# A twelve-layer decoder kernel: in the first cross attention, the output product and the second half's query projection as three one-pass products each, with the weights and the latents split by GpSimd

## What is computed

```python
x = _layernorm(x + _L0_attn_ref(...), axis=-1)
x = _layernorm(x + _L0_xattn_ref(ctx_1024, x, gamma_media, beta_media, gamma_lat, beta_lat, Wq, bq, Wkv, bkv, Wo, bo), axis=-1)
x = _layernorm(x + _L0_ffn_ref(x, router_w, w13, w2), axis=-1)      # mixture of 8 experts
```

## Time and profile before

| | before |
|---|---|
| three runs, median | 920.63 us (918.99 to 921.9) |
| profiled execution | 912.8 us, span 910.9 us |
| TensorE busy | 856.6 us, 94% |
| VectorE busy | 662.2 us, 73% |
| ScalarE busy | 572.5 us, 63% |
| GpSimd busy | 307.3 us, 34% |
| granted TensorE clock, mean | 0.989 |

### The profile page before, as it was taken

How to read it: one execution, slowest core, us unless ns; L and a number is a source line. 1 busy time by engine, 2 the same in 40 slices (tenths; PEclk the granted TensorE clock), 3 DMA queues, 4 the chain that set the end, 5 groups by cost and what they waited for, 6 DMA issues and landing times.

```text
span 910.9 us, 14508 instructions
## 1 busy us (share of the span) xinstructions
PE 856.6 (94%) x4558; PEld 561.4 (62%) x4578; DVE 662.2 (73%) x1175; ACT 572.5 (63%) x1080; POOL 307.3 (34%) x296
## 2 busy tenths in 40 slices
PE   8999999999899888989899879999999999999997
PEld 4576644776535543445545546776357888888884
DVE  3576626777779769659768766563368999999996
ACT  5356624665557556468677732334667888888886
POOL 0111004674038400019438526434001344444330
PEclk9999999999999998999999999999999999999999
DMA  9000000113000000000000061403009999999981
GB/s 358 25 1 0 0 1 18 38 50 118 0 1 2 1 1 0 1 0 2 2 0 2 2 259 52 139 24 99 1 29 217 239 245 240 244 241 244 239 222 60
DMA packets 28721, 77.82 MB, mean 85 GB/s; under 512 B 4432, under 2 KB 11856, under 8 KB 28208
## 3 DMA queue, kind: packets, MB, share of 16 engines
q1 hardware_dynamic: 27520, 74.74, 29.3%
q0 software_dynamic: 1152, 2.44, 0.8%
HBM read 72.50 MB, written 6.28 MB: 86 GB/s over the span
## 4 chain that ended last, share of the span: by engine, by line
PE 71%; DVE 16%; ACT 10%; issue 2%; DMA 1%; SPq 0%; POOL 0%; another core or an unknown queue 0%; DVEq 0%; ACTq 0%; POOLq 0%
PE ps L839 10%; PE ps L841 9%; PE ps L840 9%; PE ps L611 4%; PE ps L1228 4%; PE ps L601 3%; PE ps L624 3%; PE ps L291 2%; PE ps L1246 2%; ACT arena L1948 2%; PE ps L1550 2%; PE ps L228 2%; PE ps L1632 2%; PE ps L1603 1%; DVE arena L771 1%
## 5 line engine op out<-in xcount | busy, mean ns | idle before, releaser
L839 PE MATMUL ps<-parts 128*128 128x512 f32 x416 | 166.6, 401 | 4.0 <-DVE ps L2563 1.5
L841 PE MATMUL ps<-parts 128*128 128x512 f32 x416 | 162.1, 390 | 0.0
L840 PE MATMUL ps<-parts 128*128 128x512 f32 x416 | 161.9, 389 | 0.0
L869 ACT ACTIVATE parts<-ps 128x512 fp32r<-128x512 f32 x192 | 115.2, 600 | 54.1 <-PE ps L841 24.6
L873 DVE TENSOR_TENSOR parts<-ps,parts 128x512 fp32r<-128x512 f32 x192 | 132.5, 690 | 7.2 <-ACT parts L869 1.2
L857 POOL TENSOR_TENSOR parts<-ring,zeros 128x1024 fp32r<-128x1024 f32 (+2 forms) x36 | 51.1, 1419 | 183.1 <-PE ps L841 142.2
L2563 DVE TENSOR_TENSOR ps<-ps,arena 128x512 f32<-128x512 f32 x156 | 108.2, 694 | 3.0 <-DMA arena<-m_comb 2.1
L839 PEld LDWEIGHTS ps<-parts 128*128 128x128 f32 x416 | 78.2, 188 | 24.9 <-DVE parts L873 3.4
L2097 ACT ACTIVATE ps<-ps 128x512 f32<-128x512 f32 x156 | 90.8, 582 | 2.8 <-PE ps L841 0.4
L841 PEld LDWEIGHTS ps<-parts 128*128 128x128 f32 x416 | 78.1, 188 | 16.7
L840 PEld LDWEIGHTS ps<-parts 128*128 128x128 f32 x416 | 78.1, 188 | 16.0 <-issue 0.5
(11 more groups left out here) (479 smaller groups left out, 1535.7 us busy)
## 6 DMA issues: line engine op xcount, KB each, us to landing
arena<-m_comb SPq DMA_DIRECT2D x156, 256.0 KB, 4.7
ring<-m_in SPq DMA_DIRECT2D x20, 512.0 KB, 5.5
arena<-m_in SPq DMA_DIRECT2D x4, 1408.0 KB
pack<-pack_in SPq DMA_DIRECT2D x1, 2058.5 KB, 10.3
ring<-m_up_in SPq DMA_DIRECT2D x8, 256.0 KB, 2.7
slots_x<-empty_in SPq DMA_DIRECT2D x1, 1584.1 KB, 7.8
pack<-pack_in SPq DMA_DIRECT2D x1, 1187.0 KB, 14.8
pack<-pack_in SPq DMA_DIRECT2D x1, 1149.5 KB, 12.5
```

The costliest lines, as they stand in the source:

```text
L839: nc.tensor.matmul(dst, w_high, x_high, start=start, stop=False, skip_group_check=True)
L840: nc.tensor.matmul(dst, w_high, x_low, start=False, stop=False, skip_group_check=True)
L841: return nc.tensor.matmul(dst, w_low, x_high, start=False, stop=stop, skip_group_check=True)
L869: nc.scalar.activation(m_hh[0:rows, p], ps[0:rows, src, :], ACT.Copy).then_inc(R(t, "_hh"), 1)
```

## The change

Both products go through `mm3`. New float32r tiles are laid over the arena: `x_wo` for the split of `x_m` and later of `x_u` (8 high blocks, 8 low blocks), and sixteen `x_outs`, each with the high and low part of one head and one half of the attention output; the first of them holds the split latents of half 1 before that.

- GpSimd, before its other work: high and low part of `x_m` (two instructions of 128 x 1024), then of the latents of half 1 (two of 128 x 512). After its last copy in the wave loop: high and low part of `x_u` (two of 128 x 1024).
- TensorE: `x_project(1, ...)` and the output product issue three one-pass matmuls in place of each float32 one. The projection waits for the fourth GpSimd split, the output product for the sixth, and each of its 16 units for its own low part.
- ScalarE: 16 copies to high parts, three of them inside the last loop body, the others after it. VectorE: 16 subtractions to low parts after the loop, the bias copy after the sixth, and `center_outputs` after them all.
- The semaphore `a_zeros` of a later layer becomes the seventh count of `mid_pool`.

The diff, cut to its core: the tiles, TensorE's two products, ScalarE's high parts, VectorE's low parts, and GpSimd's splits before its first copies and after its loop.

```diff
+        x_outs = [rounded(f"x_out_{u}", (21600, 8192)[u >= 4] + T * (u % 4 if u < 4 else u - 4), T) for u in range(2 * XH)]
+        x_wo = rounded("x_wo", 25696, 2 * XH * P)
...
             def x_project(p, heads):
                 pe.wait_ge(S("norm_out"), 3 + p)
+                if p == 1:
+                    pe.wait_ge(S("mid_pool"), 4)
...
-                    mm(bank(4 + n % 4), x_m[:, h, :], x_kv[:, HB * p:HB * (p + 1), 1, :], start=True, stop=True).then_inc(S("x0_qmm"), 1)
+                    if p == 0:
+                        ins = mm(bank(4 + n % 4), x_m[:, h, :], x_kv[:, 0:HB, 1, :], start=True, stop=True)
+                    else:
+                        ins = mm3(bank(4 + n % 4), x_wo[:, h * P:(h + 1) * P], x_wo[:, (XH + h) * P:(XH + h + 1) * P],
+                                  half(x_outs[0], 0), half(x_outs[0], 1), True, True)
...
-            pe.wait_ge(S("x0_o"), 2 * B + 2)
+            pe.wait_ge(S("mid_pool"), 6)
             for p in range(2):
                 for h in range(XH):
-                    ins = mm(bank(p), x_u[:, h, :], half(x_q[:, h, :], p), start=False, stop=(h == XH - 1), skip_group_check=True)
+                    u = XH * p + h
+                    pe.wait_ge(S("x0_u"), 3 + u)
+                    ins = mm3(bank(p), x_wo[:, h * P:(h + 1) * P], x_wo[:, (XH + h) * P:(XH + h + 1) * P], half(x_outs[u], 0), half(x_outs[u], 1),
+                              False, h == XH - 1)
...
+                    elif k == 2:
+                        x_out_high(0)
+                        x_out_high(1)
+                    else:
+                        x_out_high(2)
...
+            def x_out_high(u):
+                act.wait_ge(S("x0_o"), 2 * B + 5 if u >= XH else B + 2)
+                A_(half(x_outs[u], 0), x_out(u), ACT.Copy).then_inc(S("x0_o"), 1)
...
+            for u in range(3, 2 * XH):
+                if u == 4:
+                    act.wait_ge(S("mid_pool"), 6)
+                x_out_high(u)
...
+            for u in range(2 * XH):
+                dve.wait_ge(S("x0_o"), x_out_copies(u))
+                V.tensor_tensor(half(x_outs[u], 1), x_out(u), half(x_outs[u], 0), ALU.subtract).then_inc(S("x0_u"), 1)
...
+            pool.wait_ge(S("x0_m"), 1)
+            G.tensor_tensor(x_wo[:, 0:XH * P], x_mflat, zeros[:, 0:1].to_broadcast([P, XH * P]), ALU.add).then_inc(S("mid_pool"), 1)
+            pool.wait_ge(S("mid_pool"), 1)
+            G.tensor_tensor(x_wo[:, XH * P:2 * XH * P], x_mflat, x_wo[:, 0:XH * P], ALU.subtract).then_inc(S("mid_pool"), 1)
+            pool.wait_ge(S("norm_out"), 4)
+            G.tensor_tensor(x_parts[0], x_last, zeros[:, 0:1].unsqueeze(2).to_broadcast([P, HB, P]), ALU.add).then_inc(S("mid_pool"), 1)
+            pool.wait_ge(S("mid_pool"), 3)
+            G.tensor_tensor(x_parts[1], x_last, x_parts[0], ALU.subtract).then_inc(S("mid_pool"), 1)
...
+            pool.wait_ge(S("x0_u"), 1)
+            G.tensor_tensor(x_wo[:, 0:XH * P], x_flat, zeros[:, 0:1].to_broadcast([P, XH * P]), ALU.add).then_inc(S("mid_pool"), 1)
+            pool.wait_ge(S("mid_pool"), 5)
+            G.tensor_tensor(x_wo[:, XH * P:2 * XH * P], x_flat, x_wo[:, 0:XH * P], ALU.subtract).then_inc(S("mid_pool"), 1)
```

More of the change, by code:

```diff
@@ L694, in narrow_values_scalar @@
             waits(act, t)("_vproj", 1)
-            act.wait_ge(S("a_zeros"), 1)
+            act.wait_ge(S("mid_pool"), 7)
             for p in range(2):
@@ L836, in hidden_bank, with x_out_copies, x_out @@
             return 6 + p if j < lead else 4 + 2 * (j % 2) + p
+        def x_out_copies(u):
+            return 2 * B + 1 + u + int(u >= 2) + int(u >= 3)
+        def x_out(u):
+            return half(x_q[:, u % XH, :], u // XH)
         def mm3(dst, w_high, w_low, x_high, x_low, start, stop):
@@ L1549, in x_project @@
                         pe.wait_ge(S(f"x0_q{n % 2}"), n // 2 - 1)
-                    mm(bank(4 + n % 4), x_m[:, h, :], x_kv[:, HB * p:HB * (p + 1), 1, :], start=True, stop=True).then_inc(S("x0_qmm"), 1)
+                    if p == 0:
[3 more added lines that the diff above has]
+                                  half(x_outs[0], 0), half(x_outs[0], 1), True, True)
+                    ins.then_inc(S("x0_qmm"), 1)
             def x_turn_inputs(p):
@@ L2241, in _ @@
             x_body(B // 2 - 1, True)
-            dve.wait_ge(S("x0_mw"), 5)
-            V.tensor_copy(bo, ps[:, 4, 0:4]).then_inc(S("bo"), 1)
+            for u in range(2 * XH):
+                dve.wait_ge(S("x0_o"), x_out_copies(u))
+                V.tensor_tensor(half(x_outs[u], 1), x_out(u), half(x_outs[u], 0), ALU.subtract).then_inc(S("x0_u"), 1)
+                if u == 5:
+                    dve.wait_ge(S("x0_mw"), 5)
+                    V.tensor_copy(bo, ps[:, 4, 0:4]).then_inc(S("bo"), 1)
             def center_outputs():
@@ L2605, in x_keys_values @@
                 G.tensor_copy(x_kvts[:, slot], x_kvt[:, bass.ds(b, 1), :, :].rearrange("p o s d -> p (o s) d")).then_inc(S("x0_kvts"), 1)
+            x_mflat = x_m.rearrange("p h d -> p (h d)")
+            pool.wait_ge(S("x0_m"), 1)
+            G.tensor_tensor(x_wo[:, 0:XH * P], x_mflat, zeros[:, 0:1].to_broadcast([P, XH * P]), ALU.add).then_inc(S("mid_pool"), 1)
+            pool.wait_ge(S("mid_pool"), 1)
+            G.tensor_tensor(x_wo[:, XH * P:2 * XH * P], x_mflat, x_wo[:, 0:XH * P], ALU.subtract).then_inc(S("mid_pool"), 1)
+            x_last = x_kv[:, HB:B, 1, :]
+            x_parts = [half(x_outs[0], k).rearrange("p (b t) -> p b t", b=HB) for k in range(2)]
+            pool.wait_ge(S("norm_out"), 4)
+            G.tensor_tensor(x_parts[0], x_last, zeros[:, 0:1].unsqueeze(2).to_broadcast([P, HB, P]), ALU.add).then_inc(S("mid_pool"), 1)
+            pool.wait_ge(S("mid_pool"), 3)
+            G.tensor_tensor(x_parts[1], x_last, x_parts[0], ALU.subtract).then_inc(S("mid_pool"), 1)
             for k in range(2):
@@ L2622, in _ @@
                     x_keys_values(2 * i + slot, slot)
+            pool.wait_ge(S("x0_u"), 1)
+            x_flat = x_u.rearrange("p h d -> p (h d)")
+            G.tensor_tensor(x_wo[:, 0:XH * P], x_flat, zeros[:, 0:1].to_broadcast([P, XH * P]), ALU.add).then_inc(S("mid_pool"), 1)
+            pool.wait_ge(S("mid_pool"), 5)
+            G.tensor_tensor(x_wo[:, XH * P:2 * XH * P], x_flat, x_wo[:, 0:XH * P], ALU.subtract).then_inc(S("mid_pool"), 1)
             mix_gpsimd(pool, "m0", xT, M0_CH, M0_ROWS, lambda: pool.wait_ge(S("y_ready"), 4))
             pool.wait_ge(S("y_ready"), 6)
-            G.memset(a_vflat, 0.0).then_inc(S("a_zeros"), 1)
+            G.memset(a_vflat, 0.0).then_inc(S("mid_pool"), 1)
             narrow_sums_gpsimd(pool, "x1")
```

## The result

The changed kernel took 924.3 us (median of 7 runs, 918.61 to 925.41), the kernel before, on the same chip, 920.53 us (7 runs, 918.99 to 921.9). The ratio is 1.0040 (95% interval 1.0024 to 1.0056): the change costs 2 to 5 us. Its profiled execution took 925.41 us, with a span of 923.6 us and a mean granted clock of 0.984. In a later set of runs the same kernel came to 1.0021 (1.0001 to 1.0042). Of the predicted gain of 4.3 us, 4.1 came; the loss was 6.5 us in the changed layer where 3.8 were predicted.

What follows compares the result with a forecast made beforehand. TensorE, with 71% of the chain, was taken to bound the kernel. 912.8 - 2.85 - 1.44 + 1.5 + 2.3 = 912.3 us, carried over to the median 920.1; range for 8 in 10: 916.4 to 922.4.

Steps and rivals of the forecast that it cites:

- Start collision: Before half 0's projection: GpSimd's subtraction holds up VectorE's latent scaling L2170, TensorE starts 2.15 us late; net +1.5 us.
- rival 5: Slower than before: both collisions, and TensorE's idling keeps the clock low another 3.4 us; start +3.1, about 921.7 us; chance 0.12.
- Wave collision: After 13 of 16 waves: GpSimd's `x_u` subtraction gets between VectorE's four scalings L2214 and delays what follows; +2.3 us.
- Output product: End of the layer: 16 triples of one-pass products at 0.68 us, TensorE fed without gaps; -2.85 us.
- Projection of half 1: Query projection's second half: 8 triples at 0.68 us, GpSimd's splits ready in time; -1.44 us.
- Cover behind the product: VectorE's work moved behind the low parts ends 0.6 to 1.5 us before L313, down from 11.85; cost 0.
- case 1: Likeliest rival: GpSimd gets the shared resource in both collisions, at the start and in the waves; -0.5 us, 920.1; chance 0.42.

Runs made afterwards that it cites:

- the filled gap: Changed kernel with ten throw-away products on TensorE just before its first projection, where it stands idle: 918.03 us, ratio 0.9995 to the kernel before.
- the splits alone: Kernel before with GpSimd's six splits added, their results written but not used, all products as before: 918.71 us, ratio 1.0063 to the kernel before.
- third set: Runs of the output product alone, half 1's projection alone, the gap filled, and the changed kernel again; the kernel before had a median of 919.5 us there.

## Why the prediction was wrong

The order of the causes was right and the sum was not: -0.5 us forecast, +2.4 us in the layer, and a measured time above the range. By its steps:

- **Start collision: the step that failed, in the size of a term.** The +1.5 us were 2.15 us of lateness less what the clock gives back. The lateness was right (2.09 us; the scaling at 2.63 us where 2.7 was written down, TensorE at 25.28 where 25.2). The clock gave nothing back: it took 1.22 us more. The prediction kept the low stretch of the trace before in place, from 24 to 27.4, and let TensorE start late into it. But its place and length did not stay: it began while TensorE stood still, and lasted 6.83 us, of which 5.89 lay in half 0 where the forecast had 2.2. Together +3.3 us where +1.5 stood. This is the mechanism of rival 5, which had 0.12 and whose price of +3.1 was right. Four of the five traces with the gap of 2.44 us show it (half 0 in 9.40 to 9.86 us); in the fifth, the projection alone, the low stretch was 3.41 us long and half 0 took 8.64, so that nothing was given back there either. With a gap of 0.46 us or less half 0 took 8.64 us in five traces, and 6.94 in the four in which no low stretch fell into it; the filled gap is one of these. The mean clocks of all executions go the same way: 0.9853, 0.9872, 0.9859 and 0.9863 for the four measurements with the shorter projection and the empty gap, 0.9885 to 0.9900 for all others that have them on record, those of before included. One of these others, the splits alone, has the gap too (0.9893).
- **A second low stretch near 50 us: not foreseen.** +1.0 us (the waves' 78.92 with the split of `x_u` moved against 77.91 with both moved). With the start collision and an empty gap, the clock is low for 10.24 us of the first 100 in three traces, for 6.83 in one and 3.41 in one; in the other nine for 6.82 us once, 3.41 in six, and not at all in two (the product alone, the gap filled). So this part is a tendency over traces, not one mechanism shown: the trace with the start moved had the second stretch as well.
- **Wave collision:** +2.3 us forecast, 2.15 to 2.20 measured (the splits alone and the product alone against before, the changed kernel against that with the split of `x_u` moved). Right: place (after 13 of 16 waves, in the fourteenth), mechanism (GpSimd slips between two of the four) and price.
- **Output product:** -2.85 forecast, -2.6 measured. A pass takes 0.233 us here where the expert layer's rows gave 0.227; 48 x 0.006 = 0.3.
- **Projection of half 1:** -1.44 forecast, -1.47 measured, and the four splits were ready by 28.8 us for their use at 37.7.
- **Cover behind the product:** forecast 0.6 to 1.5 us, measured 2.09; no cost, as forecast. GpSimd's L866 held up nothing.

With the start at +3.3, the second stretch at +1.0 and the product at -2.6, the sum is 3.3 + 1.0 + 2.15 - 1.47 - 2.6 = +2.4 us. The range had its upper end at 922.4 because rival 5 was added to case 1 with nothing beyond; the measured +3.8 us includes its price, the second stretch and what follows.

**What stays open.** Over the twelve measured ratios, the difference by ratio lies 1.2 us on average above the local one (from -0.3 to +3.0, each uncertain by about 2). Some of it can be read in the traces. In the eighth sublayer, the sparse expert layer, ScalarE stands idle before its first copy of an expert's result (L1315) for 1.54 us in nine of the fourteen traces, the two of before included, and for 4.2 to 6.9 us in five. There TensorE then waits before L1255: 4.0 us in the changed kernel's, 1.3 in its repetition, 2.6 with the product alone, 2.1 with the projection alone, 2.0 with the gap filled. In the changed kernel's chain of waits the profile names no releaser that it knows:

```profile
563.05 0.54 ACT arena L1306
563.60 6.88 another core or an unknown queue
...
570.50 0.29 ACT arena L1315
...
571.02 2.07 PE ps L1255 x8
```

The code there is the same in all kernels. The five traces are those of the changed kernel's first set and of the whole third set, in which the kernel before took 920.5 and 919.5 us; none of the seven traces of changed kernels from the sets in which it took 914 has the long wait. So it goes with the set of runs rather than with an edit, and the kernel before may have it too: no execution of it that took 919 us or more has a trace. What is late there isn't shown. It also makes the profiled span of the changed kernel longer (12.7 us above before's) than the medians allow (3.8 us), so the span is no measure of the change.

## What to carry to other kernels

Work that goes to GpSimd is not free where VectorE runs SBUF-to-SBUF scalings or copies on the path beside it: look up what VectorE runs there, and order the two by a wait; here one wait and one moved block turned ratios of 1.0040 and 1.0021 into 0.9990 and 0.9969. If they can't be ordered, cut GpSimd's work into short instructions, which here freed a single VectorE instruction but not a row of them. And don't price a delay of TensorE with the low stretch of the clock left where the old trace had it: a gap of 2.4 us before its work brought 6.83 us at 1.2 GHz in four of five traces.

## What the hardware showed that was not expected

A GpSimd memset, which reads nothing, holds VectorE up too. In the second trace of the kernel before (GpSimd, then VectorE):

```profile
222.73 3.51 POOL L2626 MEMSET arena<- 128x4096 f32 x1 [8.25 <-PE ps L841]
...
224.63 0.16 DVE L2270 TENSOR_TENSOR small<-pack,small 128x3 f32<-128x3 f32 x1
224.83 1.49 DVE L2272 TENSOR_SCALAR arena<-pack,small 128x128 f32<-128x128 f32 x1
...
226.62 0.28 DVE L2272 TENSOR_SCALAR arena<-pack,small 128x128 f32<-128x128 f32 x1
```

L2272 takes 0.28 us free and 1.49 beside the memset, which ends at 226.24; L2270, with two SBUF inputs of three columns, runs at 0.16 us inside it. The Trainium skill, "SBUF — State Buffer", section "SBUF: two separate sides", says that a VectorE operation with two SBUF inputs is held only against a GpSimd operation that reads SBUF; the trace agrees, as far as instructions of three columns can show it. And starting first does not keep the resource over a row of instructions: VectorE's lead of 0.30 us in the waves lasted for the first one alone.
